# A scatter of expert results moved one place forward in GpSimd's list: behind the gather seven tiles ahead instead of eight

## The chip, the cores and the metric

The kernel runs on one core of a Trainium2 chip. The metric is the device time of one execution in microseconds (us). A core has five engines with a list of instructions each: TensorE (PE, matrix products; its weight loads are shown as PEld), VectorE (DVE), ScalarE (ACT), GpSimd (POOL) and SyncE (SP, which here only issues transfers). Each engine works through its own list in order. Between engines there are only semaphores: an instruction may wait until a counter has reached a value, and may add to a counter when it is done. An instruction that waits holds up all that stands behind it on its engine.

## The reference

Six stages work on 2048 tokens of 128 numbers (4 sequences of 512): a feed-forward block, an attention, the same feed-forward block again, a mixture of experts, a second attention, and the mixture of experts again. The change concerns the two mixtures of experts alone. Of them this is what is computed (cut; `E, S, H = 8, 2, 512`):

```
logits = X @ Wg + bg
topv, topi = top_k(logits, S)            # two experts of eight for each token
w = softmax(topv);  xs = X * w           # the token, scaled by each weight
out = X
for e in range(E):
    h = silu(xs @ W1[e]) * (xs @ W3[e])
    y = h @ W2[e]
    out = out + where(topi == e, y, 0).sum()
x = x + 0.5 * out
```

## The kernel before

**Tiles.** Each token goes to two experts. The kernel sorts the 2 x 2048 pairs by expert, in two halves of tokens, and pads each expert's share to whole tiles of 128 rows. That gives HT = 23 tiles for a half and ETILES = 46 for a mixture, 92 in the program. Each of the two mixtures is a call of `moe(m)` on every engine, with m = 0 and m = 1. The tokens' normalised rows lie in DRAM (`x_rows`); results go to DRAM too (`y_rows`), and SyncE later loads them back in token order.

**One tile's way.** GpSimd gathers 128 rows by an indirect transfer into one of four buffers `XG` (L822). TensorE transposes them (L2074), ScalarE and VectorE make a high and a low half-precision part of them, TensorE multiplies by the two first matrices of the expert (L1669 to L1671, six products), ScalarE and VectorE form the gated product, TensorE transposes it (L2099), ScalarE and VectorE split it again (L1117 is ScalarE's part), TensorE multiplies by the second matrix (L2111 to L2113, twelve products, bank 5 of PSUM), ScalarE writes the result into one of four buffers `YS` (L1125, `result`), and GpSimd scatters it to `y_rows` (L830).

**The steps.** `run_tiles` walks over steps t on TensorE, ScalarE and VectorE. In step t TensorE transposes tile t, does the first products of tile t-1, the transposes of the product of tile t-2, and the second product (`down`) of tile t-3. So `down` of tile i is the last piece of step i+3, and the transpose of tile i+4 is the next instruction behind it. ScalarE's `result` of tile i stands in the same step i+3. `carried` puts other work between the steps: the rest of the feed-forward block, the second half's sorting, the next attention's weights.

**GpSimd's list.** In `moe(m)` GpSimd walks over u = 0 to ETILES + OUT_LAG - 1: first `gather(u)`, then `scatter(u - OUT_LAG)`, then its own `carried(m, u)`. A gather waits for the transpose of the tile that had its buffer before, u - 4 (semaphore `t_ps`, a TensorE count). A scatter waits for its tile's result (`y_sb`, a ScalarE count). Of `carried` three places matter, all with m = 0: at u = 9 the scale factors `rstd_of(3, 3)` (L645 to L651), which wait for VectorE's statistics; at u = 30 `attention_set` and `step_rows` (L680, L681, L714), the clearing of buffers for the next attention; at u = 42 `rstd_of(4, 0)`, again with a wait.

**What else waits for the two transfers.** TensorE's transpose of tile t waits until its gather has landed (`xg_in`). ScalarE's `result` of tile t waits until the scatter of tile t-4, which had its buffer, has landed (`y_out`). TensorE's `down` of a tile waits for the result of the tile before (`y_sb`), and its first products wait for ScalarE's and VectorE's reads of the products of the tile before. Nothing in SP's list changes its place; SP loads `y_rows` back when all 23 scatters of a half have landed.

Of the kernel before, what the change touches and what calls it, by code (L numbers as in the profile page):

```python
# [31 lines left out]
def macaron_block(nc: bass.Bass, ins, out, phases):  # L32
# [35 lines left out]
    with ctx:  # L68
# [459 lines left out]
        KEY_AT = {k: UNIT_AT[u] + at for u, unit in enumerate(EXP_UNITS) for k, at in unit}  # L528

        TLAGS = (0, 1, 2, 3)  # L530
        OUT_LAG = 8

        def run_tiles(m, stages, carried):

# [90 lines left out]
        def _(pool):  # L625
# [168 lines left out]
            def carried(m, u):  # L794

                if m == 0:
                    if u == 3:
                        rstd_of(2, 3)
                    if u == 4:
                        base_add(2, 3, b2h[:])  # L800
                    if u == 5:
                        rstd_of(3, 2)
                    if u == 9:
                        rstd_of(3, 3)
                    if u == 30:
                        attention_set()
                        step_rows(1)
                    if u == 42:
                        rstd_of(4, 0)
                else:  # L810
                    if u == 3:
                        rstd_of(5, 3)

            def moe(m):

                def gather(t):
                    if t % HT == 0:
                        pool.wait_ge(s_r_index, PARTS * m + t // HT + 1)
                        pool.wait_ge(s_x_rows[t // HT], 16 * HCH * (m + 1))
                    if t >= XRING:  # L820
                        pool.wait_ge(s_t_ps, ETILES * m + t - XRING + 1)
                    g.indirect_dma_start(XG[:, t % XRING, :], None, x_rows[t // HT],  # L822
                                         bass.IndirectOffsetOnAxis(ap=row_i[:, 0, t:t + 1], axis=0)
                                         ).then_inc(s_xg_in[t % XRING], 16)

                def scatter(t):
                    if t % HT == 0:
                        pool.wait_ge(s_r_home, PARTS * m + t // HT + 1)
                    pool.wait_ge(s_y_sb, ETILES * m + t + 1)
                    g.indirect_dma_start(y_rows, bass.IndirectOffsetOnAxis(ap=row_i[:, 1, t:t + 1], axis=0),  # L830
                                         YS[:, t % YRING, :], None).then_inc(s_y_out[t % YRING], 16)
                for u in range(ETILES + OUT_LAG):
                    if u < ETILES:
                        gather(u)
                    if u >= OUT_LAG:
                        scatter(u - OUT_LAG)
                    carried(m, u)
# [1302 lines left out]
```

## Time and profile before

| | us |
|---|---|
| three timed runs | 1015.95, 1011.63, 1015.10 |
| their median | 1015.1 |
| the profiled execution's own time | 1014.43 |
| its span (first to last instruction) | 1012.3 |
| first mixture's tiles on GpSimd (first gather to last scatter) | 361.8 to 542.4 |
| second mixture's tiles on GpSimd | 848.9 to 1001.2 |

Engine times are busy times. In a timeline row the first number is the start, in us from the start of the span, the second the duration; "x1" says that it is one instruction, and the bracket at the end gives how long the engine was idle before it and what ended that time. "remote" there means that the profile found no event of this core that fits, "issue" that it saw nothing that was waited for. The end of a TensorE product is modelled from its start. Matrix products run at full clock (granted clock 1.00) in the stretches of the second mixture from 889 us on; the mean over the span is 0.972.

### The profile page before, as it was taken

How to read it: one execution, taken by the hardware profiler on the slowest of the kernel's cores; microseconds unless marked ns; L12 is line 12 of the kernel's file. 1: busy time of each engine (PE TensorE's matmuls, PEld its weight loads, DVE VectorE, ACT ScalarE, POOL GpSimd, SP SyncE). 2: the span in 40 equal slices, each digit the busy share in tenths (PEclk: the TensorE clock that was granted, in tenths of full speed). 3: DMA queues.
4: the chain of work that ended last, by engine and by line, in shares of the span. 5: the costliest groups of instructions: out<-in, count | busy, mean ns of one | idle time of the engine just before them, and what ended most of it. 6: DMA issues, size and time to landing. Idle time of an engine off the chain costs nothing.

```text
span 1012.3 us, 33900 instructions
## 1 busy us (share of the span) xinstructions
PE 902.4 (89%) x13160; PEld 643.1 (64%) x13160; DVE 792.6 (78%) x2394; ACT 674.0 (67%) x1183; POOL 739.0 (73%) x690
## 2 busy tenths in 40 slices
PE   5889999999999779889977999999999986998894
PEld 3467677776776556556654667777777664666663
DVE  6788898888889875766656899888888987965563
ACT  6688888888877545445555777767777763555552
POOL 6789989899887745557543998878878884666662
PEclk9999999999999979899999999999999997999998
DMA  5201011010030001122111000000000000121222
GB/s 151 85 2 44 3 44 44 3 44 3 2 107 2 2 17 50 41 43 77 40 31 54 3 3 3 13 3 3 13 3 3 13 3 18 47 43 43 86 65 81
DMA packets 21118, 33.79 MB, mean 33 GB/s; under 512 B 4578, under 2 KB 10466, under 8 KB 20964
## 3 DMA queue, kind: packets, MB, share of 16 engines
q1 hardware_dynamic: 14544, 19.29, 6.0%
q0 software_dynamic: 5888, 12.07, 4.7%
q8 instruction: 110, 1.80, 0.8%
q14 instruction: 44, 0.36, 0.1%
q10 hardware_dynamic: 532, 0.27, 0.1%
HBM read 22.44 MB, written 9.18 MB: 31 GB/s over the span
## 4 chain that ended last, share of the span: by engine, by line
PE 64%; DVE 16%; issue 6%; ACT 6%; POOL 3%; another core or an unknown queue 3%; DMA 1%; SPq 0%; POOLq 0%; DVEq 0%; ACTq 0%
PE ps L1669 8%; PE ps L1860 8%; PE ps L1671 7%; PE ps L1670 7%; DVE arena L1285 4%; PE ps L1890 3%; PE ps L2099 3%; PE ps L1824 3%; PE ps L1891 3%; PE ps L1892 3%; PE ps L2113 2%; PE ps L2112 2%; PE ps L2111 2%; PE ps L1835 2%
## 5 line engine op out<-in xcount | busy, mean ns | idle before, releaser
L768 POOL TENSOR_TENSOR arena<-arena 128x1024 f16<-128x1024 f32 x190 | 344.9, 1816 | 87.2 <-ACT arena L967 76.9
L1285 DVE CUSTOM_DVE_ANT_0 arena<-ps,mask_qk 128x512 bf16<-128x512 f32 (+3 forms) x512 | 224.5, 485 | 24.7 <-PE ps L1824 23.5
L959 ACT ACTIVATE arena<-ps,lift 128x1024 f32<-128x1024 f32 (+1 forms) x192 | 186.6, 972 | 84.9 <-PE ps L1870 82.1
L1860 PE MATMUL ps<-arena 64*128 64x512 f16 (+3 forms) x1536 | 148.5, 299 | 10.2 <-ACT arena L959 6.9
L822 POOL DMA_INDIRECT arena<-x_rows,arena x92 | 91.6, 996 | 89.0 <-PE ps L2074 41.5
L1890 PE MATMUL ps<-arena 128*128 128x65 f16 x1280 | 131.8, 196 | 1.0 <-DVE arena L1309 1.0
L1891 PE MATMUL ps<-arena 128*128 128x64 f16 x1280 | 131.2, 194 | 0.0
L1892 PE MATMUL ps<-arena 128*128 128x65 f16 x1280 | 130.9, 194 | 0.0
L830 POOL DMA_INDIRECT y_rows<-arena x92 | 91.2, 992 | 48.1 <-ACT arena L1125 25.2
L1890 PEld LDWEIGHTS ps<-arena 128*128 128x128 f16 x1280 | 117.9, 98 | 9.2 <-DVE arena L1309 1.1
L1891 PEld LDWEIGHTS ps<-arena 128*128 128x128 f16 x1280 | 118.4, 99 | 0.3 <-issue 0.3
L1892 PEld LDWEIGHTS ps<-arena 128*128 128x128 f16 x1280 | 118.5, 98 | 0.0
L766 POOL CAST arena<-arena 128x1024 f16<-128x1024 f32 x124 | 103.6, 835 | 0.0
L1639 DVE SCALAR_TENSOR_TENSOR arena<-ps,arena 128x512 f32<-128x512 f32 x92 | 68.9, 749 | 29.9 <-ACT arena L1111 15.3
L1860 PEld LDWEIGHTS ps<-arena 64*128 64x128 f16 x1536 | 52.1, 94 | 53.3 <-ACT arena L959 22.5
L2111 PE MATMUL ps<-E2h,arena 128*128 x368 | 72.2, 223 | 14.7 <-ACT arena L1125 11.6
L1117 ACT ACTIVATE arena<-ps 128x512 f16<-128x512 f32 x92 | 55.2, 600 | 42.2 <-PE ps L2099 23.3
L1645 DVE TENSOR_TENSOR arena<-ps,arena 128x512 f16<-128x512 f32 x92 | 63.2, 686 | 23.2 <-ACT arena L1117 14.5
L1125 ACT ACTIVATE arena<-ps 128x128 f32<-128x128 f32 x92 | 25.6, 278 | 73.2 <-PE ps L2113 46.1
L1111 ACT ACTIVATE arena<-ps,arena 128x512 f32<-128x512 f32 x92 | 63.3, 688 | 16.4 <-PE ps L1671 11.6
L1824 PE MATMUL ps<-arena 64*128 64x512 f16 (+3 forms) x512 | 66.4, 297 | 7.8 <-DVE arena L1285 6.6
L2113 PE MATMUL ps<-E2h,arena 128*128 x368 | 72.0, 221 | 0.0
(287 smaller groups left out, 2754.0 us busy)
## 6 DMA issues: line engine op xcount, KB each, us to landing
stage<-in_L_ffn_W SPq DMA_DIRECT2D x4, 1024.0 KB, 5.3
arena<-y_rows SPq DMA_DIRECT2D x16, 256.0 KB, 3.3
x_rows<-XN SPq DMA_DIRECT2D x8, 256.0 KB, 2.0
arena<-x_rows,arena POOLq DMA_INDIRECT x92
y_rows<-arena POOLq DMA_INDIRECT x92
stage<-in_L_attn_Wkv SPq DMA_DIRECT2D x2, 512.0 KB, 7.8
out_x<-X SPq DMA_DIRECT2D x4, 256.0 KB
X<-in_L_attn_tokens SPq DMA_DIRECT2D x3, 256.0 KB, 5.4
```

The costliest lines, as they stand in the source:

```text
L766: g.tensor_copy(PH[:, b, :, cols], P32[:, :, cols]).then_inc(s_ph_pool, 1)
L768: g.tensor_tensor(PL[:, b, :, cols], P32[:, :, cols], PH[:, b, :, cols], ALU.subtract).then_inc(s_pl, 1)
L822: g.indirect_dma_start(XG[:, t % XRING, :], None, x_rows[t // HT], bass.IndirectOffsetOnAxis(ap=row_i[:, 0, t:t + 1], axis=0)).then_inc(s_ ...
L959: a_.activation(P32[:, :, UNIT_AT[u]:UNIT_AT[u] + UNIT_W[u]], ps[:, 4:6, 0:UNIT_W[u]], ACT.Exp, bias=lift[:]).then_inc(s_ex_p, 1)
L1285: v_.tensor_tensor_reduce(masked[:, x, 0:w], ps[:, 2 + x, at:at + w], mask_qk[:, CH - w:CH], 1.0, NEG, ALU.add, ALU.max, accum_out=MX[:, i ...
L1824: ins_ = mm(ps[:, 2 + x, at:at + (i + 1) * P], QKh[rows, r, 0, i * P:(i + 1) * P], QKh[rows, r, 1, 0:(i + 1) * P], start=(n_ == 0), stop=( ...
L1860: mm(ps[:, 4 + x, at:at + w], keys, queries, start=(n_ == 0 and part == 0), stop=False)
L1890: mm(ps[:, 6 + x, c:c + DH + 1], ph_, VH[:, r, k, x, 0:DH + 1], start=(k == 0), stop=False)
L1891: mm(ps[:, 6 + x, c:c + DH], ph_, VL[:, r, k, x, :], start=False, stop=False)
L1892: ins_ = mm(ps[:, 6 + x, c:c + DH + 1], pl_, VH[:, r, k, x, 0:DH + 1], start=False, stop=(k == i))
L2111: mm(dst, GH[:, g, f, :], wh, start=(f == 0), stop=False)
L2113: ins_ = mm(dst, GL[:, g, f, :], wh, start=False, stop=(f == HB - 1))
```

## The change

OUT_LAG goes from 8 to 7. GpSimd's loop now issues `gather(u)` and then `scatter(u - 7)`. Its order and what each instruction waits for by name stay; the number of turns falls from 54 to 53 in each mixture. The other four engines' lists are the same, row for row.

```
         TLAGS = (0, 1, 2, 3)
-        OUT_LAG = 8
+        OUT_LAG = 7
```

The next two pieces are GpSimd's list in the first mixture, from tile 5 on: L822 is a gather, L830 a scatter, L645 the first instruction of `rstd_of(3, 3)`. First before, then after the change.

```order
L651 TENSOR_TENSOR shift<-pw,rstd 128x4 [waits pool_step]
L822 DMA arena<-x_rows,arena 128x128 [waits t_ps] x3
L830 DMA y_rows<-arena 9984x128 [waits y_sb,r_home]
L822 DMA arena<-x_rows,arena 128x128 [waits t_ps]
L830 DMA y_rows<-arena 9984x128 [waits y_sb]
L645 TENSOR_SCALAR pw<-mv 128x4 [waits ln_mv]
```

```order
L651 TENSOR_TENSOR shift<-pw,rstd 128x4 [waits pool_step]
L822 DMA arena<-x_rows,arena 128x128 [waits t_ps] x2
L830 DMA y_rows<-arena 9984x128 [waits y_sb,r_home]
L822 DMA arena<-x_rows,arena 128x128 [waits t_ps]
L830 DMA y_rows<-arena 9984x128 [waits y_sb]
L822 DMA arena<-x_rows,arena 128x128 [waits t_ps]
L830 DMA y_rows<-arena 9984x128 [waits y_sb]
L645 TENSOR_SCALAR pw<-mv 128x4 [waits ln_mv]
```

The first scatter has moved past one gather, and three scatters instead of two stand ahead of `rstd_of(3, 3)`. From here to the last gather, each gather stands behind a scatter of a tile that is one later than before.

The second place is GpSimd's list around the clearing of the buffers (L680) at u = 30; the scatter that also waits for `r_home` is that of tile 23, the first of the second half. First before, then after.

```order
L822 DMA arena<-x_rows,arena 128x128 [waits t_ps]
L830 DMA y_rows<-arena 9984x128 [waits y_sb]
L680 MEMSET arena 128x512
L681 MEMSET arena 128x2112
L714 AFFINE_SELECT arena<-arena 128x8x62 [waits mx_set,att_set]
L714 AFFINE_SELECT arena<-arena 128x8x62 [waits mx_set] x2
L822 DMA arena<-x_rows,arena 128x128 [waits t_ps]
L830 DMA y_rows<-arena 9984x128 [waits y_sb,r_home]
```

```order
L822 DMA arena<-x_rows,arena 128x128 [waits t_ps]
L830 DMA y_rows<-arena 9984x128 [waits y_sb,r_home]
L680 MEMSET arena 128x512
L681 MEMSET arena 128x2112
L714 AFFINE_SELECT arena<-arena 128x8x62 [waits mx_set,att_set]
L714 AFFINE_SELECT arena<-arena 128x8x62 [waits mx_set] x2
L822 DMA arena<-x_rows,arena 128x128 [waits t_ps]
L830 DMA y_rows<-arena 9984x128 [waits y_sb]
```

Tile 23's scatter now stands ahead of the clearing instead of behind the gather that follows it.

## Rows read from the trace of the kernel before

**Rows 1.** The page: busy time of each engine; the chain that ended last, by engine.
```profile
PE 902.4 (89%) x13160; PEld 643.1 (64%) x13160; DVE 792.6 (78%) x2394; ACT 674.0 (67%) x1183; POOL 739.0 (73%) x690
...
PE 64%; DVE 16%; issue 6%; ACT 6%; POOL 3%; another core or an unknown queue 3%; DMA 1%; SPq 0%; POOLq 0%; DVEq 0%; ACTq 0%
```

**Rows 2.** Transposes of tiles 5 to 42, second mixture: min/median/max ns, first and last start.
```profile
L2074 PE MATMUL ps<-ident,arena x38: 279/299/309, 868.5 to 981.9; 128*128 128x128 f32 x38
```

**Rows 3.** GpSimd, second mixture's tiles, timeline from 975 us.
```profile
975.06 0.97 POOL L822 DMA_INDIRECT arena<-x_rows,arena  x1 [0.77 <-PE ps L2074]
...
978.18 0.97 POOL L822 DMA_INDIRECT arena<-x_rows,arena  x1 [0.85 <-PE ps L2074]
979.45 0.99 POOL L830 DMA_INDIRECT y_rows<-arena  x1 [0.30 <-issue]
981.25 1.09 POOL L822 DMA_INDIRECT arena<-x_rows,arena  x1 [0.81 <-remote]
982.65 0.99 POOL L830 DMA_INDIRECT y_rows<-arena  x1 [0.30 <-issue]
...
989.13 0.97 POOL L830 DMA_INDIRECT y_rows<-arena  x1 [1.68 <-ACT arena L1125]
991.65 0.97 POOL L830 DMA_INDIRECT y_rows<-arena  x1 [1.55 <-ACT arena L1125]
```

**Rows 4.** TensorE's last product of the results of tiles 37, 38, 40 and 41, timeline.
```profile
978.98 0.22 PE L2113 MATMUL ps<-E2h,arena 128*128 x1
...
981.74 0.22 PE L2113 MATMUL ps<-E2h,arena 128*128 x1
...
988.32 0.22 PE L2113 MATMUL ps<-E2h,arena 128*128 x1
...
990.84 0.22 PE L2113 MATMUL ps<-E2h,arena 128*128 x1
```

**Rows 5.** ScalarE's results of tiles 35, 37, 38, 40 and 41, timeline.
```profile
974.79 0.28 ACT L1125 ACTIVATE arena<-ps 128x128 f32<-128x128 f32 x1 [1.28 <-PE ps L2113]
...
980.34 0.28 ACT L1125 ACTIVATE arena<-ps 128x128 f32<-128x128 f32 x1 [1.05 <-PE ps L2113]
984.13 0.28 ACT L1125 ACTIVATE arena<-ps 128x128 f32<-128x128 f32 x1 [1.78 <-remote]
...
988.58 0.28 ACT L1125 ACTIVATE arena<-ps 128x128 f32<-128x128 f32 x1
991.10 0.28 ACT L1125 ACTIVATE arena<-ps 128x128 f32<-128x128 f32 x1
```

**Rows 6.** A long row of transfers, first mixture: GpSimd's first, last and next.
```profile
397.46 1.10 POOL L822 DMA_INDIRECT arena<-x_rows,arena  x1 [0.17 <-issue]
...
406.61 0.98 POOL L830 DMA_INDIRECT y_rows<-arena  x1 [0.30 <-issue]
409.27 0.97 POOL L822 DMA_INDIRECT arena<-x_rows,arena  x1 [1.68 <-remote]
```

**Rows 7.** The same stretch: the last product of tile 6 and ScalarE's result of it.
```profile
402.44 0.22 PE L2113 MATMUL ps<-E2h,arena 128*128 x1
...
408.94 0.28 ACT L1125 ACTIVATE arena<-ps 128x128 f32<-128x128 f32 x1 [3.01 <-remote]
```

**Rows 8.** GpSimd's waits, first mixture's tiles (360 to 545 us): us, times, longest.
```profile
POOL arena L822 <- PE ps L2074: 17.1, 16, 2.4
...
POOL arena L822 <- remote: 6.0, 4, 1.7
```

**Rows 9.** The same, second mixture's tiles (842 to 1003 us).
```profile
POOL arena L822 <- PE ps L2074: 24.4, 26, 2.1
...
POOL arena L822 <- remote: 7.9, 7, 1.4
```

**Rows 10.** Around the clearing of the buffers at u = 30: GpSimd, and tile 23's result.
```profile
465.24 0.28 ACT L1125 ACTIVATE arena<-ps 128x128 f32<-128x128 f32 x1 [1.39 <-PE ps L2113]
...
464.77 0.54 POOL L680 MEMSET arena<- 128x512 f16 x1
```

## Prediction

> **What bounds the kernel now.** I read the page's busy times and its chain first. TensorE is busy for 89% of the span and holds 64% of the chain; GpSimd holds 3% of it, and another 3% is time whose releaser the profile could not name [rows 1]. So a change on GpSimd is worth something only if it reaches TensorE, and the nameless share is the place to look.
>
> Next come the tiles. The transposes of tiles 5 to 42 of the second mixture start from 868.5 to 981.9 us: 37 steps in 113.4 us, 3.06 us each [rows 2]. When the last gather (981.25) is out and GpSimd only scatters, two results start at 988.58 and 991.10, 2.52 us apart [rows 5]. TensorE does the same work in both. Something costs 0.5 us a tile while gathers and scatters both run.
>
> Then GpSimd's own rows. A gather takes 0.97 us, 0.30 later the scatter begins and takes 0.99, and then it idles 0.77 to 0.85 us until a transpose is reported [rows 3]. That adds up to 3.1, and the gathers at 975.06, 978.18 and 981.25 are 3.12 and 3.07 apart: GpSimd's period is the tiles' period.
>
> Last I set TensorE's rows beside ScalarE's. The last product of a result ends at 988.32 + 0.22 = 988.54 and ScalarE starts at 988.58; 991.06 against 991.10 likewise: 0.04 us. These fall between scatters that stand alone. Where a scatter follows a gather at 0.30 us, the product ends at 979.20 and ScalarE starts only at 980.34, 1.14 later; the next ends at 981.96 and ScalarE starts at 984.13, 2.17 later [rows 4, 5]. That last start is 0.49 us after the end of the scatter (983.64), and the gather at 981.25 came 0.81 after the scatter before it. My reading: while GpSimd issues a second indirect transfer right behind a first, what TensorE has finished is reported late, until about 0.5 us after the pair's end. So there is a loop: pair, 0.5 us, report, next pair. An extreme of it is in the first mixture: 8 transfers from 397.46 to 407.59 without a pause, and tile 6's result, whose last product ended at 402.66, is taken at 408.94, 1.35 us after the row's end [rows 6, 7]. I find no row of a lone transfer that does this.
>
> **The change part by part.** No transfer is added or removed: 92 gathers and 92 scatters stay, at 0.97 to 0.99 us each. Two things move.
>
> First, the wait. Before, a scatter stood behind a gather whose transpose comes a step after its result, so its result was there (0.30 and "issue" ahead of it [rows 3]). Now `scatter(i)`, whose result is the last of step i+3, stands in front of `gather(i+8)`, which waits for the next transpose. Both are reported at nearly the same time, but the result has to pass through ScalarE. A scatter that waits starts 0.55 us after its result's start (991.10 to 991.65, 988.58 to 989.13), while the gather at 975.06 started 0.27 after the result at 974.79 [rows 3, 5]. The pair so starts 0.28 us later after each report, and becomes scatter, then gather. Queued behind it on GpSimd is that gather; behind the gather nobody who is in a hurry, since it is wanted four steps later. If the late reporting follows the pair in either order, the loop goes from 3.10 to 3.38 us.
>
> How often? Gathers waited for a report 16 + 4 times in the first mixture and 26 + 7 in the second, 53 in all [rows 8, 9]. 53 x 0.28 = 14.8 us is too much, since some results came well ahead of their gather. Going through the 76 gathers that have a scatter moved in front of them one by one (start of the result + 0.55 - start of the gather, where that is positive) gives 44 cases and 11.4 us; the first is 408.94 + 0.55 - 409.27 = 0.22 [rows 6, 7], the last 974.79 + 0.55 - 975.06 = 0.28 [rows 3, 5]. I take 11.4. From below this term could be nothing or a gain (rivals). From above: if a report comes while ScalarE has still another copy ahead of the result, the scatter waits longer; half a us for each of the 53 would be 26 us, and I keep that as the upper end.
>
> Second, the long rows of transfers. They arise after a long wait or long work on GpSimd in the first mixture, at u = 9, 30 and 42. Each has one scatter fewer after the change, since that one is issued before: 0.98 + 0.30 = 1.28 us less until TensorE is heard again. At u = 30 the clearing, which began at 464.77, now has to wait for tile 23's scatter: 465.24 + 0.55 + 0.98 = 466.77, 2.0 us later [rows 10]. Sum: -1.28 + (2.0 - 1.28) - 1.28 = -1.8 us.
>
> The tail is unchanged: behind the last gather scatters wait for results alone, and the last result is TensorE's. The first scatter at u = 7 waits for a result that it used to follow; the gather behind it has four steps of slack. The ring of result buffers has slack too, so an earlier scatter frees nothing that anyone waits for.
>
> Total: 1014.43 + 11.4 - 1.8 = 1024.0 us, against the profiled execution's own time. The median of the runs is 0.7 us above it, which I leave out.
>
> Here a rule of the Trainium skill speaks against all this. SBUF — State Buffer, "Who interferes with whom", gives DVE and GpSimd's shared port as the only contention, TensorE and ScalarE having ports of their own. By it TensorE's results would not be late through GpSimd. The trace disagrees as I read it: the 1.14 and 2.17 us against 0.04 stand beside GpSimd's pairs and nothing else that I found. By the rule the time would be that of the first rival.
>
> **The rivals.** (1) *No change, 1014 us.* The lateness comes from something else, and what the scatter waits for is hidden: a gather is issued four steps of 3.06 us before its transpose. For it: no TensorE row waits for a gather in these stretches. Against it: GpSimd's period equals the tiles' period to 0.05 us, and tiles run at 2.52 as soon as gathers end.
>
> (2) *Faster by the order, about 985 us.* The lateness belongs to a scatter right behind a gather. After the change the waiting scatter comes first and the gather second; if that order holds nothing up, 53 tiles go from 3.06 to 2.52 us: -29 us. For it: in the rows shown the late reports stand beside scatters. Against it: in a long row of both kinds they are late throughout.
>
> (3) *Faster through shorter rows, about 1005 us.* The added wait breaks rows of four transfers into pairs. The lateness was 2.17 us in a row that had just begun again and 1.14 in a pair; saving that 1.0 us in some 20 places, against the 11.4, ends at 1014.4 + 9.6 - 20 = 1004. Against it: a later scatter also lets TensorE run further ahead of GpSimd, and then the next report is already there and the row goes on.
>
> (4) *Slower by much, about 1040 us.* The upper end above: results stand behind another copy on ScalarE, 0.5 us for each of 53.
>
> **How the numbers follow.** Forecast as reckoned, 1018 to 1032 us: 0.48. Rival 4 and what lies between: 0.10. Rival 1: 0.22. Rival 2: 0.09. Rival 3: 0.11. A measurement of this kernel tells about 0.5% (5 us) from no change. Slower: 0.48 + 0.10 = 0.58. Same: 0.22. Faster: 0.09 + 0.11 = 0.20. The range reaches from 1005, the edge of rival 3, to 1038, just under rival 4; the forecast's own range is 1018 to 1032.
>
> **What would show it.** Right: in GpSimd's waits the gathers' 53 are gone and scatters wait for ScalarE's L1125 some 45 to 55 times more; the steady period is 3.3 to 3.4 us; ScalarE's results still start about 1 us after the last product. Wrong: the scatter waits, but TensorE's steps keep 3.06 us (rival 1), or fall towards 2.52 with results taken 0.04 us after the product (rival 2), or long rows with results 2 us late are gone (rival 3).

## The result and the profile after

The changed kernel takes 1019.7 us, median of 14 runs (13 of them from 1017.0 to 1021.7, and a disturbed one of 1256.7 that the comparison leaves out). The kernel before, run beside it, takes 1012.2 us (14 runs, 1009.7 to 1017.4). The ratio is 1.0059, with a 95% interval of 1.0042 to 1.0075: slower by 6 us by the ratio and by 7.5 by the medians, where 9.6 were forecast, and about at the 0.5% that a measurement can tell.

First the page of the changed kernel: its span, the busy times and the chain by engine, which answer to [rows 1].

```profile
span 1019.2 us, 33900 instructions
...
PE 903.9 (89%) x13160; PEld 643.0 (63%) x13160; DVE 791.0 (78%) x2394; ACT 673.9 (66%) x1183; POOL 739.1 (73%) x690
...
PE 59%; DVE 18%; ACT 7%; issue 6%; another core or an unknown queue 5%; POOL 3%; DMA 1%; SPq 0%; POOLq 0%; DVEq 0%; ACTq 0%
```

Every engine works as long as before. TensorE's share of the chain fell from 64% to 59%, and the nameless share rose from 3% to 5%: the chain waits more, it does not work more.

GpSimd's waits in the first mixture's tiles (360 to 545 us), against [rows 8]: us, times, longest.

```profile
POOL y_rows L830 <- ACT arena L1125: 38.9, 25, 4.6
...
POOL arena L822 <- remote: 1.0, 1, 1.0
```

And in the second mixture's (842 to 1010 us), against [rows 9].

```profile
POOL y_rows L830 <- ACT arena L1125: 45.3, 30, 2.4
...
POOL arena L822 <- PE ps L2074: 1.8, 2, 1.5
```

The 53 waits of gathers have shrunk to 3, and 55 scatters now wait for ScalarE's result (17 did before). So the wait has moved from the gather to the scatter, as the order said.

The steady period: the transposes of the second mixture from 866 us on, against [rows 2].

```profile
L2074 PE MATMUL ps<-ident,arena x34: 277/300/308, 866.7 to 976.3; 128*128 128x128 f32 x34
```

33 steps in 109.6 us are 3.32 each (3.06 before). Now the same stretch on the three engines, which answers to [rows 3 to 5]. GpSimd from 895 us on:

```profile
895.04 0.98 POOL L830 DMA_INDIRECT y_rows<-arena  x1 [1.08 <-ACT arena L1125]
896.33 0.97 POOL L822 DMA_INDIRECT arena<-x_rows,arena  x1 [0.30 <-issue]
898.37 0.98 POOL L830 DMA_INDIRECT y_rows<-arena  x1 [1.07 <-ACT arena L1125]
```

TensorE's last products of two results in it:

```profile
893.23 0.22 PE L2113 MATMUL ps<-E2h,arena 128*128 x1
...
896.18 0.22 PE L2113 MATMUL ps<-E2h,arena 128*128 x1
```

ScalarE's two results:

```profile
894.48 0.28 ACT L1125 ACTIVATE arena<-ps 128x128 f32<-128x128 f32 x1 [1.07 <-PE ps L2113]
897.81 0.28 ACT L1125 ACTIVATE arena<-ps 128x128 f32<-128x128 f32 x1 [1.45 <-PE ps L2113]
```

In these turns the loop of the prediction stands whole. The scatter at 895.04 starts 0.56 us after the result at 894.48, the gather follows 0.30 us behind it and ends at 897.30, the product that ended at 896.18 + 0.22 = 896.40 is taken at 897.81 (1.41 late, 0.51 after the pair's end), and the next scatter starts 0.56 later. The turn lasts 3.33 us. The lateness follows the pair in either order: here the gather is the second of the two.

These turns are not the rule, though. In the second mixture 10 pairs stand beside 13 rows of four transfers, each row for two tiles; before, there were 6 such rows. One of the 13, on GpSimd, TensorE and ScalarE:

```profile
961.91 0.98 POOL L830 DMA_INDIRECT y_rows<-arena  x1 [1.83 <-ACT arena L1125]
...
965.76 0.97 POOL L822 DMA_INDIRECT arena<-x_rows,arena  x1 [0.30 <-issue]
968.61 0.98 POOL L830 DMA_INDIRECT y_rows<-arena  x1 [1.89 <-ACT arena L1125]
```

```profile
963.22 0.22 PE L2113 MATMUL ps<-E2h,arena 128*128 x1
...
965.90 0.22 PE L2113 MATMUL ps<-E2h,arena 128*128 x1
```

```profile
963.48 0.28 ACT L1125 ACTIVATE arena<-ps 128x128 f32<-128x128 f32 x1 [0.61 <-PE ps L2113]
968.06 0.27 ACT L1125 ACTIVATE arena<-ps 128x128 f32<-128x128 f32 x1
```

The first product ends at 963.44 and is taken 0.04 us later, while the row runs; so the next scatter's result is there, and the row goes on to four. The second ends at 966.12 and is taken 1.94 late, 1.33 after the row's end. The row's turn lasts 6.70 us for two tiles, 3.35 each. So a report beside back-to-back transfers can be late, but need not be, and whether it comes decides whether a pair grows into a row of four.

The first mixture's long row, against [rows 6]; then ScalarE's result in it, against [rows 7].

```profile
397.90 1.10 POOL L822 DMA_INDIRECT arena<-x_rows,arena  x1 [0.17 <-issue]
...
405.75 0.98 POOL L822 DMA_INDIRECT arena<-x_rows,arena  x1 [0.30 <-issue]
408.52 0.97 POOL L830 DMA_INDIRECT y_rows<-arena  x1 [1.78 <-ACT arena L1125]
```

```profile
407.96 0.28 ACT L1125 ACTIVATE arena<-ps 128x128 f32<-128x128 f32 x1 [3.03 <-remote]
```

TensorE's last product of tile 6:

```profile
402.87 0.22 PE L2113 MATMUL ps<-E2h,arena 128*128 x1
```

Seven transfers instead of eight, ending at 406.73 instead of 407.59; tile 6's result comes 1.23 us after the row's end (1.35 before) and 4.87 us after its last product's. Around the clearing, against [rows 10]:

```profile
465.61 0.97 POOL L830 DMA_INDIRECT y_rows<-arena  x1 [1.82 <-ACT arena L1125]
466.57 0.55 POOL L680 MEMSET arena<- 128x512 f16 x1
```

The clearing begins 1.8 us later (466.57 against 464.77), behind tile 23's scatter; 2.0 were reckoned.

From the first gather to the last scatter's start the two mixtures last 178.6 and 160.0 us; before, 179.7 and 151.3. So the profile's difference of 6.9 us in the span is -1.0 in the first mixture, +8.7 in the second and -0.7 ahead of the first gather, and the forecast had been +2.6 and +7.0.

Where in the first mixture the difference arises can be read by tile. The table has the start of a tile's result in us, counted from the mixture's first gather, less the same in the kernel before. Its third column is lag7_again, the changed kernel in a second set, and its fourth wait_only_d, the order of before with the wait alone; both are described below.

| tile | changed | lag7_again | wait_only_d |
|---|---|---|---|
| 0 | +1.2 | +1.1 | +1.1 |
| 4 | +1.3 | +1.1 | +1.2 |
| 6, behind the long row of u = 9 | -0.3 | -0.3 | +1.4 |
| 23 | 0.0 | 0.0 | +3.0 |
| 29, behind the clearing | +0.1 | +0.2 | +3.3 |
| 37 | +1.3 | +1.4 | +4.8 |
| 38, behind the long row of u = 42 | -0.1 | -0.1 | +3.9 |
| 45 | -1.0 | -1.0 | +4.5 |

The results of tiles 37 and 38, first of the kernel before, then of the changed one (their first gathers are at 361.81 and 361.10):

```profile
513.42 0.28 ACT L1125 ACTIVATE arena<-ps 128x128 f32<-128x128 f32 x1 [0.34 <-PE ps L2113]
...
520.71 0.28 ACT L1125 ACTIVATE arena<-ps 128x128 f32<-128x128 f32 x1 [2.32 <-remote]
```

```profile
514.00 0.28 ACT L1125 ACTIVATE arena<-ps 128x128 f32<-128x128 f32 x1 [0.33 <-PE ps L2113]
519.89 0.28 ACT L1125 ACTIVATE arena<-ps 128x128 f32<-128x128 f32 x1 [0.92 <-remote]
```

The 1.2 us at tile 0 are there before the first scatter. They go with the clock granted to TensorE: from 361 to 375 us the mean granted clock is 0.63 in the changed kernel, as in lag7_again and wait_only_d, and 0.76 in the kernel before. It differs in two more stretches, the other way: 0.95 against 0.89 from 400 to 432 us, and 1.00 against 0.96 from 500 to 541 us. The first and the last stretch, before and after:

```profile
361.00:375.00 14.00, 9.30 (x84) 0.76 0.13 30
...
500.00:541.00 41.00, 33.95 (x285) 0.96 0.14 29
```

```profile
361.00:375.00 14.00, 10.07 (x79) 0.63 0.13 29
...
500.00:541.00 41.00, 35.51 (x297) 1.00 0.14 32
```

### The profile page after: what moved, and what is told of

It reads as the page before. It is cut to its first block, busy times and chain, and to the rows that moved or that the text cites. A ratio compares the mean times of both kernels' runs of the same rounds, so it can differ in the third digit from the quotient of the medians.

```text
span 1019.2 us, 33900 instructions
## 1 busy us (share of the span) xinstructions
PE 903.9 (89%) x13160; PEld 643.0 (63%) x13160; DVE 791.0 (78%) x2394; ACT 673.9 (66%) x1183; POOL 739.1 (73%) x690
## 4 chain that ended last, share of the span: by engine, by line
PE 59%; DVE 18%; ACT 7%; issue 6%; another core or an unknown queue 5%; POOL 3%; DMA 1%; SPq 0%; POOLq 0%; DVEq 0%; ACTq 0%
PE ps L1860 8%; PE ps L1669 8%; PE ps L1671 7%; PE ps L1670 6%; DVE arena L1285 4%; PE ps L1890 3%; PE ps L1824 3%; PE ps L1891 3%; PE ps L1892 3%; PE ps L2099 2%; PE ps L2111 2%; PE ps L2112 2%; PE ps L1835 2%; PE ps L1900 2%
## 5 line engine op out<-in xcount | busy, mean ns | idle before, releaser
L830 POOL DMA_INDIRECT y_rows<-arena x92 | 93.1, 1011 | 96.0 <-ACT arena L1125 84.3
L822 POOL DMA_INDIRECT arena<-x_rows,arena x92 | 90.5, 984 | 51.5 <-issue 25.5
L2112 PE MATMUL ps<-E2l,arena 128*128 x368 | 71.9, 220 | 0.1
## 6 DMA issues: line engine op xcount, KB each, us to landing
stage<-in_L_ffn_W SPq DMA_DIRECT2D x4, 1024.0 KB, 5.2
```

Of the source, the lines that this page charges most:

```text
L2112: mm(dst, GH[:, g, f, :], wl, start=False, stop=False)
```

## The experiments

**One thing first.** The kernel before does not have one time. In some sets of runs, on one chip each, it takes 1012 to 1019 us; in others 968 to 969; within a set all its 7 to 35 runs lie within 0.9% of each other. So each kernel below is compared with the kernel before in its own set, and the set's level is named: "1014" or "969". I did not expect this when the expectations of the first set were written. The granted clock does not explain it: 0.972 in the profile of before (1014), 0.979 in that of the changed kernel at 969, and 0.975 in scatter_sp_d, the fast kernel of a 1014 set. Over the sets, the runs of the kernel before have a mean of 0.970 to 0.971 at the upper level and 0.977 at the lower; 0.007 of 1014 us is 7 us, not 46.

### Is it the added wait, the order, or a further step? (969)

wait_only leaves the order of before and adds only the wait, ahead of the gather:

```
+    if u >= OUT_LAG:
+        pool.wait_ge(s_y_sb, ETILES * m + u - OUT_LAG + 1)
     if u < ETILES: gather(u)
     if u >= OUT_LAG: scatter(u - OUT_LAG)
```

> The order of before (gather, then scatter eight tiles back), but each gather from the ninth on also waits for the result of the tile eight back. Theory A (the added wait for ScalarE's result is the cost, since it lengthens the loop pair - report - pair by 0.28 us): as slow as the changed kernel, 1.004 to 1.009 of before, second mixture's steady period 3.33 to 3.38 us. Rival B (the cost comes from the scatter going ahead of the gather, whatever is waited for): 0.998 to 1.002.

order_only keeps the sequence of GpSimd's list, but holds each scatter until what the next gather waits for is there. The pairs become scatter, then gather, as in the change, with no new wait for a result:

```
+    if u >= OUT_LAG + 1:
+        if u < ETILES:
+            pool.wait_ge(s_t_ps, ETILES * m + u - XRING + 1)
+        scatter(u - OUT_LAG - 1)
     if u < ETILES: gather(u)
-    if u >= OUT_LAG: scatter(u - OUT_LAG)
```

> The scatter goes ahead of the gather, but it is that of the tile nine back, and both wait for the same transpose that the gather of before waits for, so no wait for a fresh result is added. Theory A: no slower than before, 0.998 to 1.002, with the pair scatter, gather holding up TensorE's reports like the pair gather, scatter; period 3.05 to 3.15 us. Rival B: slower by 0.4 to 0.9%. Rival C (only a scatter right behind a gather holds reports up): faster, 0.97 to 0.99, period about 2.6.

lag6 goes one place further:

```
-    OUT_LAG = 8
+    OUT_LAG = 6
```

> OUT_LAG 6: each scatter one more place forward. Theory A: the scatter still waits for the same result and the gather behind it for a report that came before that; the same loop, so 1.004 to 1.010 of before, period 3.33 to 3.38. Rival D (each place forward costs as much again, through the ring of gather buffers getting less slack): 1.010 to 1.015.

scatter_sp takes the scatters off GpSimd. It leaves out the sorting of the results back to tokens: SyncE stores each tile as one plain block, and GpSimd only gathers.

```
 (GpSimd)  for u in range(ETILES):
               gather(u); carried(m, u)
 (SyncE, for each tile t)
+    sp.wait_ge(s_y_sb, ETILES * m + t + 1)
+    sp.dma_start(y_rows[block * P:(block + 1) * P], YS[:, t % YRING, :]).then_inc(s_y_out[t % YRING], 16)
```

> The 92 scatters are replaced by 92 plain transfers of the result buffer on SyncE's queue, to rows by tile instead of by token (the sorting of the results back to tokens is left out; the reloads, the rest of the arithmetic and the tiles are as before). GpSimd only gathers. Theory A (GpSimd issuing two indirect transfers back to back delays TensorE's reports, and this sets the 3.1 us): period 2.5 to 2.7 us in the second mixture, results taken within 0.1 us of the last product, total 0.955 to 0.975 of before. Rival E (the lateness has another cause, as the skill page SBUF - State Buffer would have it, no contention between GpSimd and TensorE): period stays above 3.0 and the ratio above 0.99.

| label | us | before, same set | ratio [95%] |
|---|---|---|---|
| wait_only | 968.4 | 968.7 | 0.9994 [0.9982, 1.0005] |
| order_only | 968.7 | 968.7 | 1.0000 [0.9988, 1.0012] |
| lag6 | 971.4 | 968.7 | 1.0029 [1.0019, 1.0039] |
| scatter_sp | 968.8 | 968.7 | 1.0001 [0.9989, 1.0013] |

Three of the four move nothing, not even the one that takes half of GpSimd's transfers away. Only lag6 costs 2.6 us, less than either theory had said. Theory A's ratios for wait_only, lag6 and scatter_sp all missed. The traces say why: in all four, every result of tiles 5 to 37 of the second mixture is taken 0.04 us after its last product, in wait_only and order_only beside pairs and rows of GpSimd's transfers. So at this level the lateness that theory A starts from is absent, and with it the cost: this is rival 1. Nothing here separates the theories of the other level.

### The changed kernel again (1014)

lag7_again is the changed kernel, unaltered, in a new set.

> The changed kernel itself. In the call before, the kernel before took 968.7 us on its chip against 1012.2 beside the changed kernel's first runs, and taking GpSimd's scatters away changed nothing there. Theory A as now narrowed (the added wait costs time only where TensorE's reports come late beside GpSimd's pairs): if the kernel before takes about 969 us on the chip of this call, the changed one is within 0.998 to 1.003 of it; if it takes about 1012, the changed one is at 1.004 to 1.009 again. Rival F (the change costs 0.6% on any chip, through something else): 1.004 to 1.009 in both cases.

1019.0 against 1014.4 us, ratio 1.0040 [1.0020, 1.0059]. The loss is there a second time, with an interval that meets the first. Its waits are the same kind: 54 scatters wait for L1125.

### The parts once more (969)

Meant for the other level, and again at 969.

> The kernel scatter_sp again, for a chip on which the kernel before takes about 1012 us: the 92 scatters replaced by plain transfers on SyncE's queue (the sorting of results back to tokens is left out), GpSimd only gathers. On the chip of the first call, where the kernel before took 968.7 us, TensorE's reports were never late. Theory A: if the kernel before takes about 1012 us here, taking the pairs away brings this one to 960 to 975 us, ratio 0.95 to 0.965, reports on time. Rival E (on such a chip reports are late whatever GpSimd does): ratio above 0.99. If the kernel before takes about 969 us here: ratio 1.00 under both.

> The kernel wait_only again: the order of before, each gather also waiting for the result of the tile eight back. If the kernel before takes about 1012 us here: theory A (the added wait is the cost) 1.003 to 1.008, period of the second mixture above 3.3 us; rival B (the order is the cost) 0.998 to 1.002. If it takes about 969 us: 1.00 under both.

> The kernel order_only again: scatter (of the tile nine back) ahead of gather, both behind the transpose's report, no wait for a fresh result. If the kernel before takes about 1012 us here: theory A 0.997 to 1.002, period about 3.1 us; rival B 1.003 to 1.008. If it takes about 969 us: 1.00 under both.

Ratios 0.9993 [0.9981, 1.0005], 0.9984 [0.9976, 0.9993] and 0.9996 [0.9983, 1.0008], before 968.4 us. The finding of the first set stands; wait_only_b is even 0.16% faster, which the first run of the same kernel does not confirm.

### The changed kernel at the fast level (969)

> The changed kernel a third time, to tell the chips apart. Where the kernel before takes about 1014 us, theory A expects 1.003 to 1.007 as twice before; where it takes about 969 us (reports on time), 0.999 to 1.003, since the added wait then hides behind the four steps between a gather and its transpose. Rival F (cost on any chip): 1.004 to 1.007 in both.

> The kernel scatter_sp a third time: scatters replaced by plain transfers on SyncE's queue (sorting back to tokens left out). Where the kernel before takes about 1014 us, theory A: 960 to 975 us, ratio 0.95 to 0.965, TensorE's reports within 0.1 us; rival E: ratio above 0.99 and late reports although GpSimd issues no pairs. Where it takes about 969 us: 1.00.

lag7_c is the changed kernel: 968.0 against 969.0 us, 0.9991 [0.9982, 1.0000]. scatter_sp_c: 0.9999 [0.9988, 1.0010]. So the change costs 0.4 to 0.6% at one level and nothing at the other, and the trace of lag7_c shows what is missing. GpSimd's timeline:

```profile
903.84 0.97 POOL L822 DMA_INDIRECT arena<-x_rows,arena  x1 [0.30 <-issue]
905.46 0.99 POOL L830 DMA_INDIRECT y_rows<-arena  x1 [0.65 <-ACT arena L1125]
906.75 0.97 POOL L822 DMA_INDIRECT arena<-x_rows,arena  x1 [0.30 <-issue]
908.11 0.98 POOL L830 DMA_INDIRECT y_rows<-arena  x1 [0.39 <-ACT arena L1125]
```

TensorE's last products, and ScalarE's results:

```profile
904.65 0.22 PE L2113 MATMUL ps<-E2h,arena 128*128 x1
...
907.30 0.22 PE L2113 MATMUL ps<-E2h,arena 128*128 x1
```

```profile
904.91 0.28 ACT L1125 ACTIVATE arena<-ps 128x128 f32<-128x128 f32 x1
907.56 0.28 ACT L1125 ACTIVATE arena<-ps 128x128 f32<-128x128 f32 x1
```

The pairs are as tight as ever (0.30 us) and as long (0.97 and 0.99), the scatter still waits for the result and starts 0.55 us after it. But the products end at 904.87 and 907.52 and are taken 0.04 us later, the first 0.10 after a row of transfers has ended, the second in the middle of a pair. Here are its transposes and its chain:

```profile
L2074 PE MATMUL ps<-ident,arena x37: 279/281/308, 836.7 to 933.4; 128*128 128x128 f32 x37
```

```profile
PE 66%; DVE 18%; ACT 6%; issue 5%; POOL 3%; DMA 1%; SPq 0%; POOLq 0%; DVEq 0%; ACTq 0%
```

36 steps in 96.7 us are 2.69 each, and the nameless share of the chain is gone. The same program, list for list: only the lateness differs. Its span is 54.1 us shorter than that of the same kernel at 1014, and the two mixtures (148.9 and 135.1 us against 178.6 and 160.0) make all of it.

### The scatters taken off GpSimd (1014)

scatter_sp_d is scatter_sp as above, with the same part left out.

> The kernel scatter_sp once more, in the hope of a chip on which the kernel before takes about 1014 us; it has met only such on which that takes about 969 us, and there theories A and E expect the same. About 1014 us: theory A 960 to 975 us (0.95 to 0.965), reports on time; rival E above 0.99. About 969 us: 1.00. The sorting of results back to tokens is left out.

972.7 against 1019.2 us, ratio 0.9539 [0.9496, 0.9582]. GpSimd's timeline, then a last product of TensorE (L2129 in this kernel) and its result (L1141):

```profile
899.32 0.95 POOL L841 DMA_INDIRECT arena<-x_rows,arena  x1 [1.57 <-PE ps L2090]
901.84 0.95 POOL L841 DMA_INDIRECT arena<-x_rows,arena  x1 [1.58 <-PE ps L2090]
```

```profile
901.23 0.22 PE L2129 MATMUL ps<-E2h,arena 128*128 x1
```

```profile
901.48 0.28 ACT L1141 ACTIVATE arena<-ps 128x128 f32<-128x128 f32 x1
```

Each gather stands alone, results start 0.03 us after their product, and a turn takes 2.52 us: the time that the prediction had read off the last tiles [rows 4, 5]. Over tiles 5 to 42 of the second mixture, with the slower steps in it, the mean is 2.69 (3.06 before). This is the run that carries the reading. The same edit is worth 4.6% at this level and nothing, three times, at the other. Less work for GpSimd can't by itself be the reason, or it would help there too; what the edit takes away exists at one level only.

One more thing in its trace bears on this. In the first mixture a long wait still makes GpSimd send three gathers in a row. The first and the last of them, and the product and the result beside them:

```profile
393.64 1.10 POOL L841 DMA_INDIRECT arena<-x_rows,arena  x1 [0.16 <-issue]
...
396.30 0.95 POOL L841 DMA_INDIRECT arena<-x_rows,arena  x1 [0.30 <-issue]
```

```profile
395.10 0.22 PE L2129 MATMUL ps<-E2h,arena 128*128 x1
```

```profile
397.22 0.28 ACT L1141 ACTIVATE arena<-ps 128x128 f32<-128x128 f32 x1 [1.94 <-remote]
```

The product ends at 395.32 and is taken 1.90 us late, 0.03 before the row's end (397.25). Five results of that mixture are over 0.5 us late; in scatter_sp, the same program at 969, none is, beside a row of four gathers too. So this run was at the slow level like the kernel before it, it hadn't slipped to the other, and gathers alone, without any scatter, hold reports up when they stand in a row. One of the five doesn't fit: a result is 1.26 us late (398.88 to 400.14) although the transfer beside it, 398.19 to 399.14, began 0.94 us after the row. And in the steady stretch the products end 1.2 us after a gather's end, so what a lone transfer does to a product that ends beside it is hardly tested there.

### The added wait alone (1014)

wait_only_d is wait_only, at last at the level of the prediction.

> The order of before, each gather from the ninth on also waiting for the result of the tile eight back. Where the kernel before takes about 1014 us: theory A (the added wait is the cost, in whichever order the pair stands) 1.002 to 1.008 and a second mixture's period of 3.3 us or more; rival B (the scatter ahead of the gather is the cost) 0.998 to 1.002, period 3.1. Where it takes about 969 us: 1.00 under both, and the question stays open.

1026.2 against 1014.0 us, ratio 1.0119 [1.0096, 1.0143]: 12.2 us slower, and slower than the changed kernel. GpSimd's waits in the whole run (L1127 is ScalarE's result here), and the transposes:

```profile
POOL arena L822 <- ACT arena L1127: 51.9, 33, 2.4
POOL y_rows L830 <- ACT arena L1127: 24.0, 18, 4.6
```

```profile
L2076 PE MATMUL ps<-ident,arena x38: 277/299/422, 869.8 to 990.5; 128*128 128x128 f32 x38
```

37 steps of 3.26 us. The mixtures last 184.1 and 158.3 us, +4.5 and +6.9 against before: 11.4, the very sum of the first term. That match is closer than its working. Of the +4.5, 1.1 are there at tile 0, ahead of the first added wait. The forecast had 44 waits at 0.28 us; here 33 gathers wait for a result, and each starts 0.75 us after it, not 0.55, as GpSimd and ScalarE show:

```profile
960.96 0.97 POOL L822 DMA_INDIRECT arena<-x_rows,arena  x1 [1.70 <-ACT arena L1127]
```

```profile
960.21 0.28 ACT L1127 ACTIVATE arena<-ps 128x128 f32<-128x128 f32 x1 [0.91 <-remote]
```

Rows of four transfers, 6.5 us apart, have taken the place of pairs, as they have in part of the changed kernel. So this run shows that a wait put in front of a gather costs some 12 us at this level; it does not show that the price of one wait was right.

## Why the prediction was right, and where it was not

The forecast was 1024.0 us with slower the likeliest; measured are 1019.7 and 1019.0, against 1012.2 and 1014.4 before. The direction held. Of the mechanism, the lateness beside transfers in a row and the cost of the added wait held, but the simple loop of pair, report, pair is only part of what runs. The size was 2 to 5 us too large (9.6 forecast; 7.5 and 4.6 by the medians of the two sets). Step by step:

- **Lateness behind pairs.** Shown, for the 1014 level. Without pairs (scatter_sp_d) it is 0.03 us in the steady stretch and a turn there takes 2.52; where it is absent with pairs (lag7_c) tiles run at 2.69, and the change is worth nothing. In the changed kernel it is 1.03 and 1.41 us in the pairs above, and ends 0.51 after the pair's end, as reckoned. In the row of four shown it is 0.04 and 1.94; the prediction did not have both in one row.
- **The turn.** 3.33 us in pairs and 3.32 as a mean, for 3.38 forecast; the scatter starts 0.56 after the result, for 0.55. But more tiles pass in rows of four than in pairs, and in lag7_again those rows are 6.3 to 6.4 us apart, in the first run up to 6.7. Its mean over tiles 5 to 42 is 3.22, outside the 3.3 to 3.4 that were to show the reading right. That the mean came so close in the first set is in part luck.
- **How often.** The gathers' 53 waits are gone but for 3, and scatters wait 38 times more, where 45 to 55 had been said. 38 x 0.28 = 10.6 us, near the 11.4 that I took and below the 14.8 that I refused.
- **The term of the wait, 11.4 us: the step that failed in size.** By mixture it was 4.4 and 7.0. The second mixture measured +8.7, and in lag7_again, 155.8 us long, +4.5: it lies around the 7.0, and two executions of one kernel differ by 4 us there. In the first mixture, waits and clearing together had 4.4 + 0.7 = 5.1 us; between tiles 6 and 37, where they act, the changed kernel fell back by only 1.6 (1.7 in lag7_again). Up to 0.06 x 32 = 1.9 us of the missing 3.5 can be the higher clock from 400 to 432 us, an estimate; the rest stays open. In wait_only_d, whose waits cost 0.20 us more each, the same stretch cost 3.3.
- **The long rows, -1.8 us.** At u = 9 and u = 42 they gave what was forecast: -1.5 and -1.4 us (tiles 4 to 6 and 37 to 38), for -1.28 each, with 7 transfers for 8 in the row shown. Around the clearing, which begins 1.8 us later, the cost was 0.1 us (tiles 23 to 29) for the 0.7 forecast.
- **What the sum left out.** The first mixture ended at -1.0 (lag7_again, 178.7 us, -1.0) instead of +2.6. By tile it is +1.3 up to tile 4, -1.5 in the first long row, +1.6 up to tile 37, -1.4 in the last long row, and -0.9 in the last tiles. The first and the last of these go with the granted clock, which could make up to 0.13 x 14 = 1.8 and 0.04 x 41 = 1.6 us there (estimates from the rows above; no run changes the clock alone). The prediction had no term for it, and that the two nearly cancel is luck.
- **Rival 1, no change,** is what happens at 969, in the one set that timed the changed kernel there. At the 1014 level it is refuted twice by the changed kernel. I gave it 0.22 as a case of misreading; I had not thought of it as another level of the same program.
- **Rival 2,** that the order alone cures the lateness, is refuted by the rows: in the changed kernel the gather is the second of the pair and results are 1.0 and 1.4 us late.
- **Rival 3,** that rows of four break into pairs, is refuted: in the second mixture they grew from 6 to 13. What the prediction held against it is what happened, the next report is there and the row goes on.
- **Rival 4,** 0.5 us for each of 53, isn't seen: the scatter starts 0.55 us after the result all through the rows shown.
- **The Trainium skill,** SBUF — State Buffer, "Who interferes with whom", has DVE and GpSimd's shared port as the only contention. At 969 the trace of lag7_c agrees: results 0.04 us after the product beside tight pairs. At 1014 it doesn't: 46.5 us go with GpSimd's second transfer, and ScalarE starts up to 1.9 us after the product beside a row of gathers. The page speaks of ports; what is late here is the word from one engine to another, and the runs do not show through what it is held up.

**Open.** Why the same program meets late reports in some sets and none in others: chips 4 and 3 gave 1014 and 1019, chips 15 and 14 gave 968 to 969, and two sets under the label of chip 1 gave 969 and 1014, so a fixed trait of a chip isn't shown, nor is time. Whether the order alone (order_only) or a further place (lag6) gains or loses at 1014: neither was run there. Why a product that ends early in a row is taken on time in some rows and late in others. Why lag6 costs 0.3% at 969: its first mixture lasts 152.2 us against 148.9 in lag7_c, the second 135.3 against 135.1; no more is known.

## What to carry to other kernels

Where one engine's period equals the whole's, look at the gap between the end of a producer and the start of its consumer: here 0.04 us was on time, 1 us was a report held up, and the cause was on an engine that takes part in neither. On GpSimd, an indirect transfer right behind another cost 0.4 to 0.6 us a tile at the slow level (3.06 and 3.32 against 2.69); with the second transfer on another queue almost all of it was gone. Before crediting a difference to a term of the sum, follow it tile by tile: 1.2 us of it stood here ahead of the first thing that the change touches. And measure a change of 0.5% in more than one set, always beside the kernel before: here the level alone moved by 4.6%, nine times the effect, and decided whether there was one.

## What the runs showed of the hardware

- Two levels of one program, 4.6% apart (1014 and 969 us), each steady within 0.9% for a whole set of runs, at mean granted clocks of 0.970 to 0.971 and 0.977.
- At the slow level TensorE's finished work is taken 1.0 and 1.4 us late behind the pairs of indirect transfers shown, 1.9 beside a row of four or of three gathers, and 4.9 beside a row of seven, 1.23 us after the row's end; beside the start of a row of four it was also taken on time (0.04 us). With a lone transfer of 0.95 us every 2.52 us, results are on time (0.03 us), but the products there end 1.2 us after the transfer.
- A wait for a result that stands as a wait of its own in front of the gather, whose own wait is for TensorE, let the gather start 0.75 us after the result; the scatter, which waits for that result last, started 0.55 us after it.
